# Layer 4 of a four-layer model on one core: the expert tiles and the fusion of the attention branches in one block

## What is computed

```python
h = _ln(x, ln2_w, ln2_b)
...
winners = jnp.argmax(bids, axis=-1)
...
scale = win_conf / (jax.lax.stop_gradient(win_conf) + 1e-06)
hr = jnp.square(jax.nn.relu(jnp.einsum('nc,ech->enh', flat_h, K_rwkv)))
out_rwkv = jnp.einsum('enh,ehc->enc', hr, V_rwkv)
...
final = jnp.einsum('ne,enc->nc', onehot, all_out) * scale
return x + final.reshape(B, T, C)
```

```python
gate_features = jnp.concatenate([hidden_states, bn(ms_out), bn(delta_out), bn(v_direct)], -1)
hdn = jax.nn.gelu(gate_features @ fusion_w1 + fusion_b1, approximate=False)
logits = (hdn @ fusion_w2 + fusion_b2).reshape(b, L, h, 3)
wts = jax.nn.softmax(logits, -1)
o = wts[..., 0:1] * ms_out + wts[..., 1:2] * delta_out + wts[..., 2:3] * v_direct
o = o * jax.lax.rsqrt(jnp.mean(o * o, -1, keepdims=True) + 1e-05) * o_norm_w
return o.reshape(b, L, h * dv) @ Wo
```

## Time and profile before

| what | us |
|---|---|
| median of 3 runs (lowest, highest) | 2230.25 (2220.9, 2230.87) |
| the profiled execution | 2229.28 |
| its span, first to last instruction | 2227.5 |
| `tiles3`, first transposes to the last copy's end | 2045.8 to 2115.9 |
| `fusion3`, first transposes to the end of the span | 2116.7 to 2227.5 |
| POOL's gathers, first issue to last issue | 2118.2 to 2161.1 |

### The profile page before, as it was taken

The page is one execution under the profiler, slowest core; times in us unless marked ns, Lnnn a source line. Parts: engine busy times, 40 slices in busy tenths (PEclk is TensorE's granted clock), DMA queues, the critical chain, the costliest instruction groups (busy, mean ns, idle before and its releaser), DMA issues. The chain is left out here.

```text
span 2227.5 us, 45554 instructions
## 1 busy us (share of the span) xinstructions
PE 1867.1 (84%) x17730; PEld 990.0 (44%) x17736; DVE 1627.4 (73%) x2736; ACT 1200.4 (54%) x2447; POOL 643.6 (29%) x736
## 2 busy tenths in 40 slices
PE   5888877864638999999978799999779979787987
PEld 2222221532212337943343277767554434455755
DVE  7999999766889996579854855547565759776366
ACT  6999999232425884368854255557313311221475
POOL 2121120412874451134425533332124000000060
PEclk7999999977867999999988899999879989899986
DMA  7534220100732534634211112220012351430310
GB/s 180 188 86 85 58 58 1 76 18 18 180 132 52 120 55 126 178 58 79 30 24 55 56 55 75 63 73 36 11 36 83 90 168 39 133 93 13 119 53 34
DMA packets 156478, 172.01 MB, mean 77 GB/s; under 512 B 55372, under 2 KB 124950, under 8 KB 156258
## 3 DMA queue, kind: packets, MB, share of 16 engines
q1 hardware_dynamic: 142680, 144.18, 23.8%
q0 software_dynamic: 13584, 24.92, 4.4%
HBM read 95.73 MB, written 77.28 MB: 78 GB/s over the span
## 5 line engine op out<-in xcount | busy, mean ns | idle before, releaser
L590 ACT ACTIVATE a_E<-a_scores,a_nmax 128x512 f32<-128x512 f32 x512 | 343.2, 809 | 6.1 <-DVE a_nmax L523 5.3
L1180 ACT ACTIVATE a_E<-a_scores 128x512 f32<-128x512 f32 x512 | 273.7, 601 | 96.3 <-PE a_scores L1215 91.3
L523 DVE TENSOR_REDUCE a_nmax<-a_scores 128x2 f32<-128x1024 f32 x256 | 302.5, 1217 | 17.6 <-PE a_scores L605 13.7
L1084 DVE TENSOR_REDUCE a_nmax<-a_first 128x2 f32<-128x1024 f32 x256 | 295.5, 1217 | 14.5 <-PE a_first L1205 13.3
L1205 PE MATMUL a_first<-a_Kh,a_Qh 48*128 48x512 bf16 x512 | 147.5, 415 | 38.0 <-PEq L51 21.2
L618 PE MATMUL a_turn<-a_E,a_QS 128*32 128x256 f32 x2048 | 173.8, 416 | 2.3 <-DVE a_QS L533 1.8
L605 PE MATMUL a_scores<-a_Vh,a_Kh 48*128 48x512 bf16 x512 | 107.6, 418 | 74.6 <-ACT a_E L590 71.8
L1215 PE MATMUL a_scores<-a_Qh,a_Kh 51*128 51x512 bf16 x512 | 160.8, 395 | 5.0 <-PEq L51 1.9
L590 ACT ACTIVATION_READ_ACCUMULATOR a_E<-a_scores,a_nmax 128x1 f32 x512 | 164.7, 329 | 0.0
L1237 PE MATMUL a_out<-a_E,a_V 128*32 128x256 f32 x2048 | 162.2, 397 | 0.0
L3403 POOL DMA_INDIRECT XW<-in_L_KV,f_weight_rows x9 | 8.6, 953 | 389.2 <-PE a_ps_o L3843 252.7
(11 more groups left out here) (614 smaller groups left out, 4384.2 us busy)
## 6 DMA issues: line engine op xcount, KB each, us to landing
f_up<-in_L_up SPq DMA_DIRECT2D x32, 256.0 KB, 3.4
a_Kh<-a_rows_k SPq DMA_DIRECT2D x16, 384.0 KB, 6.0
a_Vh<-a_rows_v SPq DMA_DIRECT2D x16, 384.0 KB, 9.6
a_Qh<-a_rows_q SPq DMA_DIRECT2D x32, 192.0 KB
a_Kh<-a_rows_k SPq DMA_DIRECT2D x32, 192.0 KB
slots<-empty SPq DMA_DIRECT2D x8, 645.0 KB, 15.5
f_xe<-slots SPq DMA_DIRECT2D x40, 129.0 KB, 2.0
outs<-zeros SPq DMA_DIRECT2D x8, 512.0 KB, 5.8
```

Source lines behind the costliest of these rows:

```text
L523: v.tensor_reduce(nmax[:, rd % 2, r1, :, q], bank(b, u)[:], AX.X, ALU.max, negate=True).then_inc(S["max_ready"], 1)
L590: m = a.activation(E[:, u % NE, x], bank(b, u)[:, x], ACT.Exp, bias=nmax[:, rd % 2, r1, x, q:q + 1], accum_out=Z[:, rd % 2, r1, x, q:q + 1])
L1084: v.tensor_reduce(out, slot_bank(n)[:], AX.X, ALU.max, negate=True).then_inc(S["slot_read"], 1)
L1180: a.activation(E[:, u % NE, x], ps_s[n % 3][:], ACT.Exp, scale=SCALE).then_inc(S["exp_ready"], 1)
```

## The change

`tiles3` and `fusion3` become one function, `finish3`, with one block. The 9 steps of a tile (four up products, four groups of down products of the tile before, the transposes of the next one) are dealt out into 9 slots between the fusion's steps of a turn. `TILES_IN_TURN3` gives two tiles to each of the turns -2 to 1 and one tile to turns 2 and 3. The buffers in the eight banks change: the branches have one bank where there were two (`a3f_ps_t`), the hidden products one where there were two (each half is now made and read by itself), the tiles one for the transposes, one for the down products and two for the up products. The transposes of the features, the transposes of the rows and the projection share a single bank, `a3f_ps_m`. `a3f_F` has two copies. The expert rows are no longer added in `add_out`: `add_tiles` adds all of them, batch after batch, behind the last turn, and `add_out` moves to the start of a turn on DVE. POOL starts its gathers when the last tile is stored, as before.

```diff
+TILES_IN_TURN3 = {-2: 2, -1: 2, 0: 2, 1: 2, 2: 1, 3: 1}
+SLOTS3 = 9
...
+        def tile_steps(i, slot):
+            n = TILES_IN_TURN3.get(i, 0)
+            first = SLOTS3 * sum(m for j, m in TILES_IN_TURN3.items() if j < i) + n * slot
+            return [divmod(s, SLOTS3) for s in range(first, first + n)]
...
-        ps_t = [k.ps(f"a3f_ps_t{i}", [128, T]) for i in range(2)]
-        ps_f = k.ps("a3f_ps_f", [64, T])
-        ps_h = k.ps("a3f_ps_h", [128, 2, T])
+        ps_t, ps_m = k.ps("a3f_ps_t", [128, T]), k.ps("a3f_ps_m", [128, T])
+        ps_f, ps_o, ps_y = ps_m[0:64], ps_m, ps_m
+        ps_h = k.ps("a3f_ps_h", [128, T])
...
+                def tiles(i, slot):
+                    for t, j in tile_steps(i, slot):
+                        if j < NF and t < TILES3:
+                            up_product(t, j)
+                        elif NF <= j < NF + R and t:
+                            down_products(t - 1, j - NF)
+                        elif j == NF + R and t + 1 < TILES3:
+                            turn_tile(t + 1)
...
                 def turn(b, n):
                     i = 3 * b + n
-                    if i >= 2:
-                        pe.wait_ge(S["br_ready"], i - 1)
+                    if i:
+                        pe.wait_ge(S["br_ready"], i)
...
                 def turn_features(b):
                     pe.wait_ge(S["F_ready"], b + 1)
-                    if b:
-                        pe.wait_ge(S["FT_ready"], b)
+                    if b >= 3:
+                        pe.wait_ge(S["y_read"], b - 3)
...
                 def turn_out(b):
                     pe.wait_ge(S["on_ready"], b + 1)
+                    pe.wait_ge(S["FT_ready"], min(b + 4, NB))
                     if b:
-                        pe.wait_ge(S["oT_ready"], b)
+                        pe.wait_ge(S["y_read"], b)
...
                 for i in range(-2, NB + 3):
                     b_in, b_hid, b_sum, b_norm, b_out, b_add = turns(i)
+                    if b_add is not None:
+                        add_out(b_add)
                     if b_in is not None:
                         features(b_in, 0)
...
-                    if b_add is not None:
-                        add_out(b_add)
+                    tiles(i, 3)
...
+                v.drain()
+                for b in range(NB):
+                    add_tiles(b)
```

More of the change, by code:

```diff
@@ L3261, in _ @@
                         gated(b + 2)
[L3264 to L3374, removed]
@@ L3448, in layer3 @@
         E3["ye"] = k.sb("f3t_ye", [128, 2, R, C])
-        tiles3(nc, g, w, E3)
-        fusion3(nc, g, w, VT, MS, OT, E3, out)
+        finish3(nc, g, w, VT, MS, OT, E3, out)
 RING3 = 3
@@ L4048, in _ @@
             def _(pool):
+                for t in range(3, TILES3):
+                    pool.wait_ge(E["y_done"], t - 2)
+                    E3["fetch"](pool, t)
                 for i, s in enumerate(E3["stored"]):
@@ L4115, in _ @@
                         turn(b_in, 0)
+                    tiles(i, 0)
+                    if b_in is not None:
                         turn(b_in, 1)
+                    tiles(i, 1)
                     if b_hid == 0:
@@ L4132, in _ @@
                         project(b_out)
+                    tiles(i, 8)
             @block.scalar
@@ L4179, in out_turned, with scaled, positive, tile_out @@
                     a.copy(oT[:], ps_o[:]).then_inc(S["oT_ready"], 1)
+                def scaled(t):
+                    a.wait_ge(E["x_turned"], t + 1)
+                    if t >= 2:
+                        a.wait_ge(E["h_done"], NF * (t - 1))
+                    a.activation(xT[:, t % 2], ps_tx[:], ACT.Identity, scale=scale, bias=bias).then_inc(E["xT_ready"], 1)
+                def positive(t, f):
+                    i = NF * t + f
+                    a.wait_ge(E["h_done"], i + 1)
+                    if t >= 2:
+                        a.wait_ge(E["y_done"], t - 1)
+                    a.activation(hr[:, t % 2, f], ps_th[i % 2][:], ACT.Relu).then_inc(E["relu_ready"], 1)
+                def tile_out(t):
+                    a.wait_ge(E["y_done"], t + 1)
+                    if t >= 2:
+                        a.wait_ge(E3["stored"][t % 2], t // 2 * 16)
+                    a.copy(ye[:, t % 2].rearrange("p q c -> p (q c)"), ps_ty[:]).then_inc(E["y_ready"], 1)
+                def tiles(i, slot):
+                    for t, j in tile_steps(i, slot):
+                        if j < NF and t < TILES3:
+                            positive(t, j)
+                        elif j == NF + R - 1 and t:
+                            tile_out(t - 1)
+                        elif j == NF + R and t + 1 < TILES3:
+                            scaled(t + 1)
+                scaled(0)
                 for i in range(-2, NB + 2):
@@ L4198, in _ @@
                     if b_hid is not None:
-                        hidden(b_hid)
+                        hidden(b_hid, 0)
+                    tiles(i, 5)
+                    if b_out is not None:
+                        out_turned(b_out)
+                    tiles(i, 6)
+                    if b_hid is not None:
+                        hidden(b_hid, 1)
+                    tiles(i, 7)
                     if b_sum is not None:
                         squares(b_sum)
+                    tiles(i, 8)
             @block.vector
```

128 lines of the change are left out of this document (94 added, 34 removed).

## The result

The kernel after took 2245.87 us at the median of six runs (2239.61 to 2250.16), the kernel before 2229.88 over its six (2220.9 to 2231.62): **a ratio of 1.0068, 95% interval 1.0048 to 1.0088**. The forecast was 2231, with a range of 2218 to 2244: too low by 15 us, and the time lies just above the range. The profiled execution of after took 2250.16 us, its span 2248.1 at a mean clock of 0.901. Its last block starts at 2048.80, 3.0 us later than in the profile before. The code ahead of it is the same, and profiled executions of this program differ there by several us (the starts lie between 2038 and 2052). So I compare stretches inside the block, which sum to 199.3 us after and 181.7 before.

What follows compares the result with a forecast made beforehand. PE was taken to bound the tiles, a ring between DVE and PE the fusion. From 2045.8, stretches of 87.1, 27.9, 40.4 and 28.1 us end the span at 2229.3; with 1.8 around it, 2231 us, range 2218 to 2244.

Steps and rivals of the forecast that it cites:

- stretch A: Turns -2 to 1, eight tiles interleaved: 75.8 us of PE work, 2.5 slow start, 8.8 waits; 87.1 us.
- The slow start: Start of the block's tiles: the first eight records and first copies cost 2.5 us extra, unchanged.
- The waits on `f3t_xT`: PE waiting in the tiles' turns, some eight times for 0.7 to 1.2 us.
- B: Turns 2 and 3: two full turns, last up products, down products of tiles 7 and 8, waits; 27.9 us.
- C: Turn 4 to the last logits' end, no tiles left, shared bank: 40.4 us, where it was 40.1.
- The slower rival: Turn 4 to last logits: PE stays at low clock, 48.6 us; time 2239, or 2248 with doubled waits; chance 0.2.
- the ring: Turns from 4: shared bank chains sums of squares, addition, transposes, logits, softmax; 11.4 us between logits at full clock.
- Stretch D: Last logits to the end: sums of squares 7.0, projection chain 10.2, expert-row additions 8.4, last store 2.5; 28.1 us.
- the balance: Whole block: interleaving gives 5.4 us by turn 4, later stretches take it back; span ends 1.8 us later than before.

Runs made afterwards that it cites:

- the last kernel: Kernel after with hidden products in one piece, next tile's transposes earlier, expert-row additions in DVE's waits, separate banks from turn 4: 0.9928 to before, 2212.5 us.
- separate banks: Kernel after with rows' transposes, projection and branches' transposes on the tiles' free banks from turn 4 on: 1.0051 to before, 2241.84 us.
- the kernel with the pair: Kernel after with both feature products side by side again, the second half's products in the logits' bank: 1.0014 to before, 2230.62 us.
- the early transposes: Kernel after with the next tile's transposes sixth instead of ninth of a tile's nine steps: 1.0085 to before, 2243.18 us.
- the moved additions: Kernel after with the 32 additions of expert rows moved from the end into DVE's waits from turn 6 on: 1.0063 to before, 2239.4 us.

## Why the prediction was wrong, by its own steps

**The step that failed** is the price of the hidden products. The forecast read 2.87 us from the earlier trace rows as the price of four products, carried it into all eight turns, and charged the split with nothing but a wait for the gelu, 1 to 1.5 us in stretch A. It never asked what the feature products' 1.13 us for four instructions meant beside the 1.88 for the four with 128 rows, although the 512 columns are the same. One half is 2.01 us. The rest follows:

- A, +4.3: three turns with hidden products, 3 x 1.15 = 3.5. The slow start took 2055.28 - 2048.80 = 6.5 us for 3.15 us of work, 0.8 more than the 2.5 taken. The waits on `f3t_xT` and the relu came to 6.1 in place of the 8.8 with the gelu's. That leaves 2.6 us. The up and down products, which take 3.5 to 3.8 us in pieces between other steps where 3.43 and 3.57 were taken, are 1.9 of it; the rest I haven't traced.
- B, +4.5: two turns, 2.3, and of the other 2.2 most, about 1.7, is the low clock behind the branch's wait in turn 3 (15.50 us at 0.89). With the pair back and the clock at 1.00, B took 27.54 in the last kernel; the forecast was 27.9.
- C, +7.0: three turns. The rows of their hidden products, grouped (busy us, mean ns of one, idle before), come to 20 us, at a mean clock between the two levels, where three times 2.87 is 8.6 at the full clock:

```profile
L4035 PE MATMUL a3f_ps_h<-XT,a3f_W1x 128*128 128x512 f32 x12 | 10.2, 945 | 1.7 <-ACT a3f_hid L4121 1.7
L4038 PE MATMUL a3f_ps_h<-a3f_FT,a3f_W1f 32*128 32x512 f32 x12 | 9.8, 909 | 0.0
```

  In turn 4 the doubled durations start behind the gelu's wait of 1.49 us between the halves, in turn 6 behind the 1.9 us for the addition to `X`. The forecast charged PE with a wait for the gelu in A only. The logits start 15.1, 12.6 and 14.0 us apart, where 12.0, 13.0 and 11.2 were forecast.

A second, smaller slip is in C: the clock of 0.86 of the kernel before holds to 2195 only the earlier trace rows. To the last logits' end, the stretch that C compares with, it is 0.76, by the windows of the kernel before:

```profile
2166.16:2206.27 40.11, 33.89 (x163) 24.92 (x161) 29.57 (x68) 29.09 (x42) 0.00 (x0) 0.76 0.07 25
```

**The slower rival** had the size right (2239 to 2248) and the mechanism wrong. It laid the low clock and the long turns to the ring, but with separate banks C keeps its length (47.13 us) and its low clock (0.67), and it forecast 16.4 us between logits, more than any turn took.

**What held.** Stretch D, 28.1 us, with its parts. PE in the end stretch of after, which answers to the earlier trace rows, waits 3.83 us for DVE where the kernel before waited 5.57:

```profile
2227.67 1.08 PE L4057 MATMUL a3f_ps_m<-ident,a3f_o 128*128 128x128 f32 x4 [3.83 <-DVE X L4263]
2229.43 2.08 PE L4063 MATMUL a3f_ps_m<-a3f_Wo,a3f_oT 128*128 128x128 f32 x8 [0.67 <-ACT a3f_oT L4144]
2232.38 1.09 PE L4057 MATMUL a3f_ps_m<-ident,a3f_o 128*128 128x128 f32 x4 [0.87 <-DVE X L4263]
```

and the additions, forecast at 8.4 us from the earlier trace rows, are one block that waits for no gather:

```profile
2237.05 8.49 DVE L4270 SCALAR_TENSOR_TENSOR X<-f_got,f_weight,X 128x128 f32<-128x128 f32 x32
```

The gathers (lines of POOL and ACT, grouped: busy us, mean ns, idle before) took 34.2 us for 32 and were hidden. The forecast had them 2 us longer than before, and they weren't (34.42 in the earlier trace rows). The table loads stayed 24:

```profile
L3971 POOL DMA_INDIRECT f_got<-outs,f_get x32 | 34.2, 1070 | 55.4 <-DMA outs<-f3t_ye 46.0 <-issue 9.4
...
L4121 ACT ACT_TABLE_LOAD x8 | 10.3, 1283 | 1.5 <-PE a3f_ps_h L4038 1.4
L4126 ACT ACT_TABLE_LOAD x8 | 10.3, 1283 | 0.1
L4138 ACT ACT_TABLE_LOAD x8 | 10.3, 1283 | 0.1
```

And the balance held in its total: without the split, interleaving gives about as much as the waits, the shared bank and the additions at the end take away (1.0014). That it comes to 2231 is in part luck. The block was forecast at 183.5 us and takes 180.1 in the trace of the kernel with the pair: turns 2 and 3 are 2.0 us longer than forecast, and turn 4 to the last logits' end is 4.4 shorter (35.97 for 40.4).

**What stays open.** Why the early transposes show 7 us in a trace, and the moved additions 8.6 us at its end, and neither shows anything in the times when it stands alone. And how much of the 10 to 15 us between after and the kernel with the pair is the products themselves and how much the clock: 8 turns at 1.15 to 2.2 us give 9 to 18.

## What to carry to other kernels

A group's duration belongs to its neighbours as well as to its instructions: before a change splits a group or puts work between its parts, divide its time by its count, compare with a like row, and ask what overlap a short one hides. Two products that ran side by side on TensorE here did so only while they stood next to each other: keep such a pair together, and if a bank is wanted for it, lend one from a step that is idle then. And where one engine's work covers a shared resource, measure the resource again once that work has shrunk.

## What the runs showed of the hardware that I had not expected

Two products of f32 over 32 rows each and 512 columns, which read different groups of 32 rows, write different banks and stand next to each other, run at the same time: 1.06 us for both. With the same rows for both it is 1.91, a factor of 1.8, and with another product between them 2 x 1.05.

The Trainium skill (TensorE: Matmul & The Clock Gate, "Packing small matmuls — row/col tiling") says that products at different row positions of the array run concurrently, that a pack of them lasts hardly longer than one, and that the position follows from where the operands start, at partition 0, 32, 64 or 96. The trace agrees, 1.06 us for the pair, and the code of before has just this form, `rows = slice(32 * c, 32 * c + 32)`, without a word on it. The prediction would have needed that rule to read the earlier trace rows rightly.

And the time for which PE stays at 1.2 GHz behind a like wait isn't fixed: turn 3, the same 87 instructions and the same 0.73 us, took 20.41 us at a mean clock of 0.67 in one execution and 15.50 at 0.89 in another, and 18.74 at 0.73 in a second execution of the kernel after itself.
